# Attention logits of the second graph layer on TensorE, its edge phase in pieces of eight columns

## The reference, cut to what matters

```python
h_edge = ((atom[src] + bond) @ W).reshape(-1, H, D)      # H = 2, D = 64, bond: [200000, 64]
h_node = (atom @ W).reshape(-1, H, D)
el = jnp.einsum('ehd,hd->eh', h_edge, attn_l)
er = jnp.einsum('nhd,hd->nh', h_node, attn_r)
s = el + er[dst]
s = jnp.where(s > 0, s, 0.2 * s)
smax = jax.ops.segment_max(s, dst, num_segments=N)
ex = jnp.exp(s - smax[dst])
denom = jax.ops.segment_sum(ex, dst, num_segments=N)
alpha = ex / denom[dst]
ft = jax.ops.segment_sum(h_edge * alpha[..., None], dst, num_segments=N)
```

## Time and profile before

| what | us |
|---|---|
| time, median of 3 runs | 12229.82 (12229.76 to 12237.26) |
| profiled execution, time | 12260.86 |
| its span | 12259.2 |
| busy in the span: PE, DVE, ACT, POOL | 2784.4, 4720.5, 3336.0, 6796.8 |
| edge phase 1, first gather to the start of the last | 2845.85 to 5017.91 |
| its DVE, ACT, POOL and PE busy in that stretch | 1462.47, 569.98, 1647.26, 0 |
| node phase 1 begins | 5064.60 |

### The profile page before, as it was taken

One profiled execution on the slowest core, in us unless ns is written; L12 is line 12 of the kernel. 1 busy time (PEld: TensorE's weight loads), 2 busy tenths in 40 slices (PEclk: granted clock), 3 DMA queues, 4 the chain that ended last, 5 costly groups with the idle time before them and its releaser, 6 DMA issues. The chain is left out here.

```text
span 12259.2 us, 65857 instructions
## 1 busy us (share of the span) xinstructions
PE 2784.4 (23%) x15715; PEld 2527.7 (21%) x15715; DVE 4720.5 (39%) x6666; ACT 3336.0 (27%) x4637; POOL 6796.8 (55%) x6997
## 2 busy tenths in 40 slices
PE   2000000011000000134444444444233333333333
PEld 1000000010000000033434334333232322322233
DVE  3455555555666666432222222222231111111113
ACT  0222222233222222122222222222232232232231
POOL 6666666657777777544444444444434544544543
PEclk6555555555555555577777766666655555555556
DMA  6233333312333333222222222222112222222221
GB/s 270 91 98 98 95 98 95 98 45 77 95 97 97 94 97 93 66 76 76 75 76 75 76 76 75 76 76 76 39 42 55 62 62 55 63 62 56 61 62 52
DMA packets 366488, 982.76 MB, mean 80 GB/s; under 512 B 163829, under 2 KB 173583, under 8 KB 351653
## 3 DMA queue, kind: packets, MB, share of 16 engines
q1 hardware_dynamic: 135572, 667.06, 14.6%
q0 software_dynamic: 224608, 290.88, 11.2%
q10 hardware_dynamic: 6192, 23.73, 0.5%
HBM read 582.50 MB, written 398.69 MB: 80 GB/s over the span
## 5 line engine op out<-in xcount | busy, mean ns | idle before, releaser
L771 POOL DMA_INDIRECT se<-x_table,edge_ix x1512 | 1429.2, 945 | 1883.5 <-PEq L1343 1408.0
L771 POOL DMA_INDIRECT comb<-x_table,edge_ix x1512 | 1430.6, 946 | 1481.4 <-DMA edge_ix<-in_src 1021.9
L771 POOL DMA_INDIRECT g<-x_table,edge_ix x1512 | 1590.5, 1052 | 508.1 <-issue 508.1
L771 POOL DMA_INDIRECT qv<-qv_table,edge_ix x1484 | 1408.6, 949 | 679.5 <-issue 445.9
L889 DVE TENSOR_TENSOR_SCAN edge_val<-edge_bank,edge_val 128x464 f32<-128x464 f32 (+1 forms) x715 | 687.4, 1031 | 2485.4 <-ACT edge_val L1597 2478.9
L1565 PE MATMUL h_ps<-w_hidden,edge_comb_t 97*128 97x128 f32 x3136 | 706.2, 397 | 1931.8 <-ACT edge_comb_t L1592 1219.1
L899 ACT ACTIVATE edge_sums<-edge_val 128x1904 f32<-128x1904 f32 (+3 forms) x219 | 1107.1, 5055 | 0.0
L1454 DVE TENSOR_TENSOR edge_product<-mk_ps,edge_q_now 128x256 f32<-128x256 f32 x392 | 166.4, 424 | 2380.9 <-ACT edge_msg L1393 2352.9
L1565 PEld LDWEIGHTS h_ps<-w_hidden,edge_comb_t 97*128 97x128 f32 x3136 | 619.7, 294 | 2007.9 <-ACT edge_comb_t L1592 1274.2
L1353 PE MATMUL mk_ps<-w_mk,edge_se_t 128*128 128x128 f32 x3136 | 544.0, 328 | 1675.9 <-issue 1430.9
L1353 PEld LDWEIGHTS mk_ps<-w_mk,edge_se_t 128*128 128x128 f32 x3136 | 480.9, 234 | 1727.5 <-issue 1443.1
(11 more groups left out here) (417 smaller groups left out, 9146.5 us busy)
## 6 DMA issues: line engine op xcount, KB each, us to landing
sums<-edge_sums SPq DMA_DIRECT2D x56, 1848.0 KB
sums<-edge_sums SPq DMA_DIRECT2D x55, 1792.0 KB, 6.6
sums<-edge_sums SPq DMA_DIRECT2D x56, 1008.0 KB
sums<-edge_sums SPq DMA_DIRECT2D x55, 924.0 KB, 3.7
edge_k<-k_edges SPq DMA_DIRECT2D x56, 896.0 KB
edge_bond<-in_edge_attr SPq DMA_DIRECT2D x56, 896.0 KB
edge_eh<-in_edge_attr SPq DMA_DIRECT2D x56, 896.0 KB
edge_qr<-in_edge_attr_n SPq DMA_DIRECT2D x56, 896.0 KB
```

Source lines behind the costliest of these rows:

```text
L771: e.indirect_dma_start(self.gather_into(u, j), None, self.gather_from, bass.IndirectOffsetOnAxis(ap=now[:, j:j + 1], axis=0))\
```

## The change

**The logits.** In the search phase, the product of W's two halves with `attn_l` gives a matrix `el_w` of 128 x 4. Its rows are 64 features of one column and 64 of the next, its columns are two columns times two heads. A pair of columns of summed rows (128 partitions x 128 numbers) is transposed by PE, moved from PSUM to SBUF by ACT, and multiplied by `el_w` on PE into the PSUM tile `logits`. DVE reads the logits from there. The product and the sum over features on DVE (L1212, L1215) and the tile `product` are gone.

**The pieces.** A chunk is taken in four pieces of 8, 8, 8 and 4 columns. For a piece DVE waits for its two (the last: one) groups of four gathers and adds the bond features (`add`). PE transposes 4 (the last: 2) pairs (`turn`), ACT moves them (`move`), PE multiplies (`multiply`). `bond_ps`, `t_ps` and `tile_t` have two buffers each, used in turn by the pieces. The first piece of the next chunk is added by DVE between a chunk's weighting and its scans, and moved by ACT between the exponentials and `lay_out`.

**The last chunk.** It is cut behind 16 columns: scores, exponentials, weighting and scans are done for columns 0 to 15, then for 16 to 27, and the first part is laid out and stored (`lay_out_cut`, `store_cut`, as in edge phase 2) while the second is worked on. The rounds of DVE and ACT are a loop of 27 and a last round written out.

POOL's program and SP's rounds stay as they are, but for the extra store.

```diff
         g = [ctx.enter_context(nc.sbuf_tensor(f"g{b}", [P, J, FD], F32)) for b in (0, 1)]
         ph = EdgePhase(p, 1, ctx, p.x_tables[0], lambda b, j: g[b][:, j, :], J // QUAD)
         bond = [ph.sb(f"bond{b}", [P, J, FD]) for b in (0, 1)]
-        product = ph.sb("product", [P, J, 2, FD])
-        bond_banks = ph.ps("bond_ps", [P, 4, 512])
+        tile_t = [ph.sb(f"tile_t{u}", [P, QUAD, P]) for u in (0, 1)]
+        bond_banks = [ph.ps(f"bond_ps{u}", [P, 512]) for u in (0, 1)]
+        t_banks = [ph.ps(f"t_ps{u}", [P, 512]) for u in (0, 1)]
...
+            def turn(i, b, k):
+                first, end = pieces[k]
+                m = b * each + k
+                e.wait_ge(added, at(i, per, m + 3))
+                e.wait_ge(moved, at(i, per, m + 1))
+                for j in range(first, end, 2):
+                    last = e.transpose(t_ps[k % 2][:, (j - first) // 2, :],
+                                       g[b][:, j:j + 2, :].rearrange("p j f -> p (j f)"), p.ident[:, :])
+                last.then_inc(turned, 1)
+
+            def multiply(i, b, k):
+                first, end = pieces[k]
+                e.wait_ge(moved, at(i, per, b * each + k + 3))
+                for j in range(first, end, 2):
+                    last = e.matmul(logits[:, j:j + 2, :].rearrange("p j h -> p (j h)"),
+                                    tile_t[k % 2][:, (j - first) // 2, :], p.el_w[:, :], start=True, stop=True)
+                last.then_inc(scored, 1)
...
+            def chunk(i, b, following):
+                for k in range(1, each):
+                    move_and_lay(i, b, k)
+                for k in (0, 1):
+                    lay_bond(*following, k)
+                ph.exponentials(e, i, b, decay)
+                move_and_lay(*following, 0)
+                ph.lay_out(e, i, b)
...
+            chunk(i, 0, (i, 1))
+            move_and_lay(i, 1, 1)
+            ph.exponentials(e, i, 1, cut_decay(0), 0)
+            for k in (2, 3):
+                move(i, 1, k)
+            e.wait_ge(cut_summed, 1)
+            ph.lay_out_cut(e, lambda to, of: e.activation(to, of, ACT.Copy))
+            ph.exponentials(e, i, 1, cut_decay(1), 1)
+            ph.lay_out_first(e)
...
-                    ph.wait_gathered(e, i, b)
-                    e.wait_ge(bonded, at(i, 2, 1 + b))
-                    e.tensor_tensor(g[b][:, :, :], g[b][:, :, :], bond_ps[:, :, :], ALU.add)
-                    e.drain().then_inc(bond_used, 1)
-                    e.tensor_tensor(product[:, :, :, :], bcast(g[b][:, :, :], 2, 2),
-                                    bcast(attn_l, 1, J), ALU.mult)
-                    e.drain()
-                    e.tensor_reduce(dots, product.rearrange("p j h d -> p h j d"), AX.X, ALU.add)
-                    e.drain()
...
+            def chunk(i, b, following):
+                for k in range(1, each):
+                    add(i, b, k)
+                score(i, b, each, slice(0, J), rows_of(i, b, J))
+                ph.carry_values(e, i, b)
+                ph.running_softmax(e, i, b)
+                ph.wait_weights(e, i, b)
+                rows_now = g[b][:, :, :].rearrange("p j d -> p d j")
+                for n in range(2):
+                    e.tensor_tensor(ph.values(b)[:, n, :, :], rows_now, bcast(ph.weight[:, n, :], 1, FD), ALU.mult)
+                e.drain().then_inc(ph.rows_free[b], 1)
+                add(*following, 0)
+                ph.wait_decay(e, i, b)
```

More of the change, by code:

```diff
@@ L141, in __init__ @@
         self.w1_heads = keep("w1_heads", [2 * FD, FD])
-        self.attn_l = keep("attn_l", [P, 2, FD])
+        self.el_w = keep("el_w", [P, 4])
         self.attn_r = keep("attn_r", [FD, 2])
@@ L1165, in edge_phase_1 @@
     rows = 17
+    wide = 2 * QUAD
+    pieces = [(first, min(first + wide, J)) for first in range(0, J, wide)]
+    per, each = 2 * len(pieces), len(pieces)
     with ExitStack() as ctx:
@@ L1193, in _ @@
             chained.gpsimd(e)
+        @block.tensor
+        def _(e):
+            e.sem_inc(scored, 2)
+            def turn(i, b, k):
[14 more added lines that the diff above has]
+                last.then_inc(scored, 1)
+            with e.Fori(0, ph.rounds) as i:
+                for b in (0, 1):
+                    for k in range(each):
+                        turn(i, b, k)
+                        multiply(i, b, k)
+            chained.tensor(e)
@@ new lines, in add, with score @@
+            def add(i, b, k):
+                first, end = pieces[k]
+                for c in range(first // QUAD, end // QUAD):
+                    ph.wait_part(e, i, b, c)
+                e.wait_ge(bonded, at(i, per, b * each + k + 1))
+                rows_now = g[b][:, first:end, :]
+                e.tensor_tensor(rows_now, rows_now, bond_ps[k % 2][:, 0:end - first, :], ALU.add)
+                e.drain().then_inc(added, 1)
+            def score(i, b, upto, now, er_now):
+                e.wait_ge(scored, at(i, per, b * each + upto + 2))
+                e.tensor_tensor(joint[:, :, now], logits[:, now, :].rearrange("p j h -> p h j"),
+                                er[:, er_now, :].rearrange("p j h -> p h j"), ALU.add)
+                e.drain()
+                e.tensor_scalar(damped[:, :, now], joint[:, :, now], 0.2, None, ALU.mult)
+                e.drain()
+                e.tensor_tensor(ph.score[:, :, now], damped[:, :, now], joint[:, :, now], ALU.max)
```

151 lines of the change are left out of this document (88 added, 63 removed).

## The result

The changed kernel takes 12888.85 us (median of 4 runs, 12885.46 to 12895.38); the kernel before took 12233.03 on the same chip (4 runs, 12229.76 to 12237.26). The ratio is 1.0539 [1.0527, 1.0552]: slower, by 656 us, 39 us above the forecast of 12850 and inside its range. The profiled execution's span is 12893.6 us, 634.4 more than before.

What follows compares the result with a forecast made beforehand. POOL's gathers bound edge phase 1 at 39.2 us a chunk; late PE-to-ACT handoffs would make it 50. Profiled 12260.9 + 599 (loop) + 25 (end) = 12885, its time 31 above the median, so 12850 us; range 12400 to 13200.

Steps and rivals of the forecast that it cites:

- POOL is the bound and DVE's saved work worth nothing in the loop: Edge phase 1: gathers explain the 39.2 us period; the 7.8 us of DVE work saved a chunk is hidden behind them.
- The period, 50 us: Edge phase 1's chunk cycle after the change: late PE-to-ACT handoffs raise it to 50 us; POOL stands still 15 us.
- The loop, +599: Edge phase 1, first gather to last: 2771 us for 2172 before, from 53 periods of 50 us.
- The end, +25: Last landing to node phase 1: 69 us for 44, DVE being a chunk behind, with the cut last chunk.
- Gathers of a burst at 1.25 us: POOL in edge phase 1: 28 gathers at 1.25 us, 35 us a burst, the pace of the phase's first chunks.
- three times PE to ACT: New handoffs of a chunk in edge phase 1; free if all delays, including one PE to DVE, stay below 10.7 us.
- rival A: Edge phase 1, prompt handoffs: period stays 39.2 us, only the end gains 13 us, 12217 us; chance 0.11.
- The range: Whole kernel: late handoffs with a cycle of 43 to 56 us give 12400 to 13200 us; chance 0.80.
- Rival B: Edge phase 1: without L1212 and L1215 gathers run faster, 4.2 us a chunk over 47 chunks, 12020 us; chance 0.06.
- C: Edge phase 1: piece 1 also seen late and gathers at 1.39 us, cycle 62 us, 13490 us; chance 0.03.

Runs made afterwards that it cites:

- PE alone: Kernel before, with 28 transposes of the identity on PE in every chunk of edge phase 1, awaited only by `Chained` behind the loop: 12306.69 us, ratio 1.006.
- the kernel with pauses: Changed kernel, in edge phase 1 POOL waits behind every eighth gather until the group of four it ends has landed: 12373.49 us, ratio 1.0117.
- the probe: Kernel before, three PE-to-ACT handoffs a chunk of edge phase 1, ten identity transposes each: 12504.2 us, ratio 1.0222; with four each 12232.52 us.

## Why the prediction was right, and where its reason was not

- **POOL is the bound and DVE's saved work worth nothing in the loop**: so it is. DVE lost 7.8 us of work a chunk and got 22.7 us of waiting.
- **The period, 50 us**: 50.6. Of the chunk's steps the first, the scans, the layout and the last move "5 us behind the end of the gathers" (4.5 in the chunk shown) are as told. The single delays were not 10 and 10 us but 5.7 and 9.6 there. Over the 56 chunks the move of piece 2 is 4.6 us late in the median (at most 5.7) and that of piece 3 12.0 (at most 19.4). That the steps fall where the forecast has them is partly luck: piece 2 is turned 3 us later than told (20.9 us into the burst for 18) and its delay is 4 us shorter, and the two errors cancel. Since the last move is tied to the end of the burst, the size of the first delay hardly mattered.
- **The loop, +599**: +627 (2798.8 for 2172.1 before). The gathers span 5647.07 - 2848.26 = 2798.8 us for a forecast of 2771. 53 periods at 0.6 us more explain it.
- **The end, +25**: +30. Without the cut it is +27.5 (one profile each), so the cut, which the sum let save time, saves none.
- **Gathers of a burst at 1.25 us**: as forecast; with the period set by DVE it is worth nothing.
- **The step that was wrong is what makes PE late.** The prediction counted handoffs, "three times PE to ACT", each with a delay of 7 to 25 us some 14 us into an unbroken run. Three handoffs of four transposes cost nothing in a run that is never broken, three of ten transposes cost 273 us: it is the number of PE instructions beside the gathers. The age of the run alone is not the condition either, since PE alone went at full pace until 83 us into the phase's run. My rows of phases 2 and 3 and of the node phase could not tell the two apart, since all of them have many PE instructions (in node phase 1, the lightest, 62 rows in 5065 to 5188 us, which is 20 in 39 us). That my number came out right is luck in part. The delays were taken from phase 3, and its load is not close: a chunk has 56 PE instructions there (28 transposes and 28 products, 84 rows in the trace), twice the 28 of the changed kernel (42 rows). What helped is that the last move is tied to the end of POOL's burst, and the burst's length was known. The "over 130" that rival A gives for phase 2 fits no way of counting: it is 112 instructions (56 transposes, 56 products) or 168 rows.
- **The range** leaned on the bounds of that row and holds. Rival A's conditions came true in the kernel with pauses, whose end is A's to 0.3 us. Rival B is refuted: the gathers did get faster, but it isn't L1212 and L1215 that slow them. They run at 1.25 us beside L1212 where POOL has stopped not long before, and all through the phase on the chips of 9000 us; 1.39 is the pace of a run that is some 200 gathers old and never broken, on the others. C did not come up.
- By a rule that the prediction set against the rows, the Trainium skill (SBUF — State Buffer, Who interferes with whom), TensorE and ScalarE wait for nobody. On the chips of 9000 us the moves are as prompt as it says; on those of 12231 us PE does one transpose in 2.8 us and the trace names nothing that it waits for. Whether that is a wait for SBUF, which is what the rule is about, no run shows.
- **Open**: what makes PE late. It is one condition of the chip together with POOL's unbroken issuing. Between 3000 and 4400 us SP's issue of a store takes 1.40 us in 33 of 36 cases of the kernel before there and 0.36 in all 40 on the others, and gathers in a long run take 1.39 for 1.25, so it is not PE's alone. And the pauses free SP as well: with three a chunk, on a chip of 12231 us, 33 of 34 of these issues take 0.4 us or less. A resource that all of them share, that the gathers load at 1.25 us but can hold only at 1.39, and on which work piles up until POOL stops, would fit all of this: the first prompt instructions of a burst and of the phase, the pauses, PE's slowness for a while behind the run, and the gathers' own change of pace. That is an argument and not shown; nothing in the traces names such a resource. Open is also why PE, a long way behind, stayed slow for 26 us when the gathers had ended.

## What to carry to other kernels

On chips like those of 12231 us, work that is moved to TensorE beside an unbroken run of indirect gathers can't be priced by the length of its rows. Count its instructions: here 12 a period of 39 us were free. What more of them cost depends on who waits: 18 more cost 273/56 = 4.9 us a chunk in the probe, ten products came to 6.4 us in the changed kernel, and PE alone took 2.8 us for each. If the phase is bound by the gathers, the move can win nothing in the loop anyway, so ask first what the freed engine was waiting for. Where PE must work there, stop POOL for the landing of a group of gathers now and then: three stops a chunk, of 1.7 to 4 us idle, gave back 515 of 656 us; whether fewer would do is not shown, and where nothing was late each stop cost 1.4 us. And compare kernels on the same chip only.

## What the runs showed of the hardware that I had not expected

- Chips of the same kind differ by a quarter of the time on this kernel: 12231 us on two of those used for the experiments, 9000 on two others. From the first gather to the last, the four edge phases have 2861 of the 3230 us between them (phases 1 to 3 go at 35 us a chunk against 39.2, 62.0 and 54.5); the rest is mostly in the node phases. The gathers' packets take equally long on both (0.081 and 0.082 us).
- In the slow condition PE gets through one transpose in 2.8 us (720 in 2015 us) with no wait in the record, in steps of 0.70 us; behind the gathers 758 take 84.57 us.
- It needs no long queue of gathers: in the changed kernel the last packet of one is done 2.1 us behind its issue in the median. With three stops a chunk (1.7, 1.7 and 4.0 us) nothing is late.
- The trace can show PE's instructions as done 24 us before anyone sees their result. The wait is then put down to "remote", to "issue" or to a store that has nothing to do with it; only the row of the engine that waits can be trusted.
